# Two edits in a graph-network kernel: every fourth o unit leaves PSUM by DVE, and the fourth weight comes from one accumulating pass

## What is computed

```python
diff = (region_relation_weights[..., None] - mean_relation) ** 2      # 4 kernels
w = jnp.exp(-0.5 * diff / (1e-14 + precision_relation ** 2))
w = w / jnp.sum(w, axis=-1, keepdims=True)
ws = jnp.sum(w, axis=2)                    # one number per row and kernel
weighted = ws[..., None] * neighbourhood_features[:, :, None, :]
out = jnp.einsum('bknd,nod->bkno', weighted, W)
...
x = _layernorm(x + _L0_gnn_ref(...))
```

## Time and profile before

| | |
|---|---|
| median of 3 runs | 908.11 us (906.81 to 911.09) |
| the profiled execution | 911.44 us |
| its span from first to last instruction | 909.7 us |
| busy in the span | PE 754.8, DVE 761.7, ACT 772.7, POOL 693.6 us |
| mean granted TensorE clock | 0.935 |

### The profile page before, as it was taken

The page is one execution under the profiler, slowest core; times in us unless marked ns, Lnnn a source line. Parts: engine busy times, 40 slices in busy tenths (PEclk is TensorE's granted clock), DMA queues, the critical chain, the costliest instruction groups (busy, mean ns, idle before and its releaser), DMA issues.

```text
span 909.7 us, 12461 instructions
## 1 busy us (share of the span) xinstructions
PE 754.8 (83%) x3922; PEld 354.9 (39%) x3922; DVE 761.7 (84%) x1636; ACT 772.7 (85%) x761; POOL 693.6 (76%) x788
## 2 busy tenths in 40 slices
PE   1544458799999999999999999999999989994650
PEld 1211123344444444444444444444444434443640
DVE  1999988979999999999999999999999932327991
ACT  5999989989999999999999999999999811118971
POOL 6699999998888888888888888888888220002996
PEclk9866669899999999999999999999999999998895
DMA  8789887887797879877877798889766200898997
GB/s 231 206 256 254 208 225 175 211 196 197 197 239 193 190 183 239 205 190 187 232 186 187 194 243 198 194 199 234 186 163 162 47 1 0 314 359 318 333 391 284
DMA packets 262677, 191.18 MB, mean 210 GB/s; under 512 B 210002, under 2 KB 210258, under 8 KB 261074
## 3 DMA queue, kind: packets, MB, share of 16 engines
q1 hardware_dynamic: 262466, 190.38, 76.9%
q10 hardware_dynamic: 144, 0.00, 0.0%
HBM read 91.52 MB, written 48.50 MB: 154 GB/s over the span
## 4 chain that ended last, share of the span: by engine, by line
DVE 45%; POOL 22%; ACT 14%; PE 10%; issue 5%; DMA 2%; SPq 0%; DVEq 0%; POOLq 0%; ACTq 0%
DVE wgt L825 17%; DVE ps_t L857 17%; DVE x_in L844 5%; PE ps_z L1012 5%; ACT ps_t L593 4%; ACT ps_t L591 4%; POOL adj_cut L453 4%; PE ps_o L1028 3%; POOL adj_in L448 2%; POOL x_turn L464 2%; POOL x1p L490 2%; POOL adj_cut L451 2%; PE ps_t L1028 2%; POOL adjT L548 2%; DMA w_sel<-w_planes 1%
## 5 line engine op out<-in xcount | busy, mean ns | idle before, releaser
L1012 PE MATMUL ps_z<-adjT,x1p 128*128 128x512 f16 x1536 | 345.0, 381 | 0.0
L997 PE MATMUL ps_h<-w0T,x_turn 128*128 128x512 f16 x768 | 195.5, 409 | 74.0 <-DVE x_in L844 55.9
L857 DVE TENSOR_TENSOR ps_t<-ps_t,wgt 128x1024 f32<-128x1024 f32 x192 | 235.9, 1229 | 22.4 <-ACT ps_t L587 17.8
L825 DVE SCALAR_TENSOR_TENSOR wgt<-wgt,ps_t 128x1024 f32<-128x1024 f32 x192 | 224.8, 1215 | 17.4 <-ACT ps_t L593 17.2
L1012 PEld LDWEIGHTS ps_z<-adjT,x1p 128*128 128x128 f16 x1536 | 150.3, 98 | 181.6 <-issue 4.6
L576 ACT ACTIVATE wgt<-adj_in,neg_mu 128x1024 f32<-128x1024 f32 x192 | 205.8, 1136 | 8.2 <-POOL adj_in L448 8.2
L582 ACT ACTIVATE wgt<-wgt 128x3072 f32<-128x3072 f32 x64 | 176.5, 2758 | 0.0
L1028 PE MATMUL ps_o<-zT,w_sel 128*128 128x512 f16 x684 | 159.4, 383 | 6.7 <-DMA w_sel<-w_planes 6.6
L997 PEld LDWEIGHTS ps_h<-w0T,x_turn 128*128 128x128 f16 x768 | 75.8, 103 | 183.6 <-issue 95.6
L453 POOL TENSOR_TENSOR adj_cut<-adj_in,adj_cut 128x1024 f16<-128x1024 f32 x64 | 136.6, 2134 | 5.3
L1028 PEld LDWEIGHTS ps_o<-zT,w_sel 128*128 128x128 f16 x684 | 67.1, 99 | 89.8 <-DMA w_sel<-w_planes 8.5
(11 more groups left out here) (219 smaller groups left out, 859.8 us busy)
## 6 DMA issues: line engine op xcount, KB each, us to landing
adj_in<-in_adj_dram SPq DMA_DIRECT2D x64, 512.0 KB, 4.0
x_in<-in_x_dram SPq DMA_DIRECT2D x64, 256.0 KB, 4.3
x_spill<-x_in SPq DMA_DIRECT2D x28, 512.0 KB, 3.3
out_spill<-o_stage SPq DMA_DIRECT2D x49, 256.0 KB, 2.9
w_sel<-w_planes SPq DMA_DIRECT2D x8, 1024.0 KB, 5.9
adjT<-x_spill SPq DMA_DIRECT2D x6, 1024.0 KB, 12.6
out_dram<-adjT SPq DMA_DIRECT2D x6, 1024.0 KB, 7.2
adjT<-out_spill SPq DMA_DIRECT2D x4, 1024.0 KB, 13.1
```

The lines of the kernel that those rows point to most:

```text
L825: v.scalar_tensor_tensor(out=wgt[:, m % 2, j, :], in0=wgt[:, m % 2, j, :], scalar=SUM_SCALE / W0_SCALE, in1=tot, op0=ALU.mult, op1=ALU.mul ...
L857: v.tensor_tensor(tot, tot, wgt[:, n % 2, j, :], ALU.add).then_inc(dve_tot, 1)
L997: last = te.matmul(ps_h[:, n % 2, :], xT[:, n % 2, left, c, :], w0T[:, right, c, :], start=(c + i == 0), stop=(c == C - 1 and i == 2))
L1012: last = te.matmul(ps_z[:, u % 2, :], x1p[:, b % 2, left, t, k * P:(k + 1) * P], adjT[:, b % 2, right, t, half * HALF:(half + 1) * HALF], ...
```

## The change

Two edits. First, o units 3, 7, ..., 47 (12 of 64) are copied from `ps_o` to `o_stage` by a DVE `tensor_copy` in a new function `take_o`, placed between the low half of z and the mean and variance; ACT leaves them out. All who waited for ACT's copy of such a unit (its statistics, its store, the next o product) wait for DVE's. Second, the fourth row sum comes from one pass over three elements, `sum(whole - wsum)` with `whole` = (NR / W0_SCALE, 0, 0), whose accumulator is read into `wsum`; both its tensor inputs lie in SBUF.

```diff
-        rest = sb("rest", [P, 1])
+        whole = sb("whole", [P, NK - 1])
+        spare = sb("spare", [P, NK - 1])
...
+        def taken_by_dve(u):
+            return u % G == G - 1 and u < KEPT
+
+        def taken(u):
+
+            if taken_by_dve(u):
+                return dve_o, u // G + 1
+            return act_o, u + 1 - min(u + 1, KEPT) // G
...
-                    sp.wait_ge(act_o, u)
+                    sp.wait_ge(*taken(u - 1))
...
-                if 0 <= u < TILES:
+                if 0 <= u < TILES and not taken_by_dve(u):
                     k = u % G
                     act.wait_ge(pe_o, u + 1)
...
+            v.memset(whole[:, 1:NK - 1], 0.0)
+            v.memset(whole[:, 0:1], NR / W0_SCALE)
...
+            def take_o(u):
+                dve.wait_ge(pe_o, u + 1)
+                wait(dve, o_stored[1], u // 2 * 16)
+                dve.wait_ge(dve_ostat, u)
+                v.tensor_copy(out_unit(u), ps_out(u)).then_inc(dve_o, 1)
+
...
-                v.tensor_reduce(rest[:], wsum[:, m % 2, 0:NK - 1], AX_X, ALU.add).then_inc(dve_rest, 1)
-                dve.wait_ge(dve_rest, m + 1)
-                v.tensor_scalar(wsum[:, m % 2, NK - 1:NK], rest[:], -1.0, NR / W0_SCALE,
-                                ALU.mult, ALU.add).then_inc(dve_ws, 1)
+                v.scalar_tensor_tensor(out=spare[:], in0=wsum[:, m % 2, 0:NK - 1], scalar=-1.0, in1=whole[:],
+                                       op0=ALU.mult, op1=ALU.add, accum_out=wsum[:, m % 2, NK - 1:NK]).then_inc(dve_ws, 1)
...
+                if 0 <= n - O_LAG - 1 < TILES and taken_by_dve(n - O_LAG - 1):
+                    take_o(n - O_LAG - 1)
...
-                wait(pe, act_o, u - 1 if u > KEPT + 1 else u)
+                ahead = u - 2 if u > KEPT + 1 else u - 1
+                if ahead >= 0:
+                    pe.wait_ge(*taken(ahead))
```

More of the change, by code:

```diff
@@ L148, in gnn_program @@
         act_last, dve_out = sem("act_last"), sem("dve_out")
-        dve_tot, dve_ws, dve_rest, dve_y, dve_stat, dve_mv = (
-            sem(f"dve_{k}") for k in ("tot", "ws", "rest", "y", "stat", "mv"))
-        dve_z, dve_ostat, dve_omv, dve_sumT = (sem(f"dve_{k}") for k in ("z", "ostat", "omv", "sumT"))
+        dve_tot, dve_ws, dve_y, dve_stat, dve_mv = (
+            sem(f"dve_{k}") for k in ("tot", "ws", "y", "stat", "mv"))
+        dve_z, dve_o, dve_ostat, dve_omv, dve_sumT = (sem(f"dve_{k}") for k in ("z", "o", "ostat", "omv", "sumT"))
         dve_routing, dve_route = sem("dve_routing"), sem("dve_route")
@@ L662, in relu @@
                 if chunks[0] == 0:
-                    wait(act, act_o, TILES if n < 2 else 0)
+                    if n < 2:
+                        act.wait_ge(*taken(TILES - 1))
                     wait(act, *landed(o_back, n))
@@ L812, in o_stats @@
                 else:
-                    dve.wait_ge(act_o, u + 1)
+                    dve.wait_ge(*taken(u))
                 v.bn_stats(o_stat[:, b % 2, k, half, :], ps_out(u) if u == TILES - 1 else out_unit(u)).then_inc(dve_ostat, 1)
```

## The result

The changed kernel took **921.77 us** in the median (919.68 to 926.28), the kernel before 909.6 in the runs beside it: ratio 1.0147 (95% interval 1.0106 to 1.0189), 1.5% slower. The profiled execution took 922.19 us with a span of 920.4, against 911.44 and 909.7. From here on a line number is that of the kernel whose rows are shown; in the changed kernel Ln is L601, Exp L603, the row sums L844, the new pass L849, `weighted` L861, the adds L874, the copy on DVE L825, and POOL's lines stand ten higher than before.

The account below looks back on a forecast made before the run. The prediction took a ring through ACT's Ln and Exp and DVE's sums and adds as the bound. Six rounds +14.8, m = 15 +1.3, last step -0.2: +15.9 us on 908.11 gives 924.0 us, own range 919 to 928.

Parts of the forecast that it names:

- DVE's ring: Loop of Ln and Exp on ACT, then row sums, fourth sum, `weighted` and adds on DVE; period 10.95 us.
- 0.12 us of room: ACT's own path is 0.12 us shorter than the loop of waits, so shortening DVE gains at most that per ordinary step.
- The copy: Each of 12 DVE copies of an o unit takes 0.67 us and adds 0.60 to DVE's stream.
- hides behind Exp: DVE's wait for Exp covers 0.32 us of a copy: 0.28 remains at u % 8 = 3, all 0.60 at u % 8 = 7.
- SP and PE behind the copy: Unit's store and transpose of x in SP's queue, and next o product, come late behind the copy; counted at nothing.
- The saving by length: The new pass in place of two instructions for the fourth sum saves DVE 0.18 us a step, range 0.11 to 0.19.
- The exclusion: The pass, with two SBUF inputs, waits until 0.12 us before the end of POOL's current instruction; 0.40 us for m even.
- The eight steps: Step changes over eight m: 4 x 0.22 + 2 x 0.39 + 0.39 + 0.42 = 2.47 us, six such rounds.
- router steps: Steps putting the pass a little later into POOL's L451; only -1 us in the forecast's range.
- The margin at m % 8 = 5: The pass misses POOL's longest instruction by 0.11 us; otherwise 2.03 us waits six times, 936 us, chance 0.17.
- The term of +1.3 for m = 15: At m = 15 the pass meets POOL's L453 at its start and waits 1.89 us where 0.57 was counted.
- counting steps 0 to 14 at nothing: Early steps cost nothing, since ACT's 3.53 us stall at their end, waiting for PE, takes up a late DVE.

Follow-up runs that it names:

- one_input_alone: Changed kernel with all copies back on ACT and the three-element pass as an accumulating tensor_scalar with one SBUF tensor input: 903.38 us, ratio 0.9927 to the kernel before.
- copies_only: Changed kernel with the old reduce and tensor_scalar put back, so only the 12 copies on DVE remain: 913.49 us, ratio 1.0056 to the kernel before.
- pool_later_before: Kernel before, with one small unused POOL operation put ahead of each normalization: 908.92 us, ratio 1.0011 to the kernel before.
- pass_only: Changed kernel with all copies back on ACT, keeping the pass with two SBUF inputs: 921.02 us, ratio 1.0126 to the kernel before.
- one_input_both: Changed kernel, copies kept, with the pass as an accumulating tensor_scalar with one SBUF tensor input: 904.55 us, ratio 0.9947 to the kernel before.
- quarters_two_inputs: Changed kernel with each second DVE copy (units u % 8 = 7) cut into four pieces: 932.88 us, ratio 1.0254 to the kernel before.

## Why the prediction was right

The forecast of 924.0 us (own range 919 to 928) was met with 921.77, by the mechanism named. The closeness of the two numbers is in part luck: the forecast added 15.9 us to a median of 908.11, and the kernel before measured 909.6 beside the changed one. The change itself is 12.2 us, three quarters of what was forecast. By its steps:

- **DVE's ring bounds the loop, ACT has 0.12 us of room.** Right. Ln waited for the adds 52 times instead of 13, and one_input_alone ran into ACT at 10.83.
- **The copy.** The length was right at 0.67 (0.680 measured; the lower end, 0.54, is out). In the stream it adds 0.65, not 0.60: in copies_only the steps of u % 8 = 7 are 0.65 us longer and those of u % 8 = 3 are 0.29 (0.60 and 0.28 forecast). That it hides behind Exp in one kind and not in the other is shown by these two numbers. SP and PE behind the copy did not matter: six rounds of these two steps, 6 x 0.94 = 5.6, are the whole 5.67 of the loop.
- **The saving by length.** Where the pass does not wait, `weighted` starts 269.09 - 268.77 = 0.32 us after it, 0.49 before: 0.17 saved, 0.18 forecast.
- **The exclusion.** Right for three elements as for L871's 1024: the pass was held in 0.77, 1.04 and 2.13 us instructions of POOL alike until their end, and not with one input; "whatever POOL is doing" went too far, as L487 above shows. The Trainium skill (SBUF — State Buffer, "Who interferes with whom") states it for a DVE instruction with two SBUF inputs beside a GpSimd one that reads SBUF, and that one with at most one such input does not contend, outside VectorE's 2-port modes; 0.52 to 0.70 against 0.154 us agree with both, while the pass of 0.16 us inside L487, which reads SBUF too, does not agree with the first. The pass began about 0.15 us before the end of POOL's instruction (0.53 long and ending 0.01 behind it, of which 0.16 is its own), not 0.12, so a wait is 0.36 where 0.40 was forecast.
- **The eight steps.** Measured against forecast, from the starts of Ln in both traces:

| m % 8 | steps | pass us | longer by | forecast |
|---|---|---|---|---|
| even | 4 | 0.52 | 0.18 | 0.22 |
| 7 | 1 | 0.70 | 0.36 | 0.39 |
| 3 | 1 | 0.54 | 0.23 | 0.39 |
| 1, copy | 1 | 0.40 | 0.36 | 0.39 |
| 5, copy | 1 | 0.16 | 0.47 | 0.42 |

  They sum to 2.14, forecast 2.47. Of the 0.33 missing, 0.16 is in the four even steps and 0.16 in m % 8 = 3, where router steps between the sums already made the step 11.26 long and the pass meets L461 later; it was counted as an ordinary one and named only in the range. The margin at m % 8 = 5 was 0.05 us, not 0.11, since the copy was 0.05 dearer in the stream.
- **The ends.** The term of +1.3 for m = 15 did not come. At m = 15 the pass met L461, not L463, and waited 0.54:

```profile
200.54 0.70 DVE L849 SCALAR_TENSOR_TENSOR spare<-wsum,whole 128x3 f32<-128x3 f32 x1
200.19 1.04 POOL L461 TENSOR_SCALAR adj_cut<-adj_in 128x1024 f16<-128x1024 f32 x1
```

  The stall of the earlier trace rows, by which that meeting was placed, was absent: the step of m = 13, 14.46 us long in the kernel before, is 10.82 to 11.09 in all nine other profiles, pool_later_before (10.95) among them. So it seems to belong to that execution, and was no ground for counting steps 0 to 14 at nothing. PE's first o product, which had waited 4.40 us for its weights before, began 2.12 us earlier. Timelines of PE, before and after:

```profile
179.18 0.61 PE L1028 MATMUL ps_o<-zT,w_sel 128*128 128x512 f16 x1 [4.40 <-DMA w_sel<-w_planes]
```

```profile
177.06 2.75 PE L1049 MATMUL ps_o<-zT,w_sel 128*128 128x512 f16 x12
```

  Six rounds of 2.14 would be 12.8 us; the loop grew by 12.36, with 0.6 less for the passes of m = 40 and 41, which POOL did not hold. Forecast were 14.8 + 1.3; smaller steps by 6 x 0.33 = 2.0 and the term of m = 15 are most of the difference.

**Open.** Ln of m = 15 stands between 191.98 and 196.03 us in the ten profiles, in no order with the edits (196.03 before, 194.80 in pool_later_before, 192.69 in pass_only, 191.98 in one_input_both). With one profile of each kernel the effect of an edit on steps 0 to 14 can't be told from what varies there between executions. The prediction's zero for these steps is neither shown nor refuted, though passes of 0.16 to 1.42 us stand in them too. The 2 us by which the medians of one_input_both go beyond its loop are not explained either. What follows the loop varies as well, from 183.2 to 188.2 us, the longest in one_input_alone.

## What to carry to other kernels

Before two short instructions of DVE are merged into one, count the tensors it reads from SBUF: with two of them it waited here for the instruction that POOL had in flight, of 0.62 to 2.13 us, however few elements it had itself (one record of 0.71 us let it pass), and that wait is inside its record and counted as busy time. Compare its mean with its minimum, and lay its rows beside POOL's; a form with an accumulator start in place of the second tensor got here, from the same edit, 0.7% faster instead of 1.3% slower. And before an instruction is moved to another engine, ask what the receiver waits for: on a ring whose two engines differ by 0.12 us, work taken from the one gives nothing and work put on the other costs its whole length wherever no wait hides it.

## What the runs showed that I had not expected

- Three elements took 2.02 us (quarters_two_inputs), over twelve times their own 0.16, and 0.2 us of lateness in one step of eight cost 11 us in all.
- More work on POOL made a kernel 16.4 us faster (921.02 to 904.58), by nothing but phase.
- Where the pass was held, it never ended more than about 0.02 us behind the POOL instruction that held it; by its own 0.16 us it is let in some 0.15 us before that record ends.
